# Rows of the modulated layer norm in two vector passes, and the last attention groups' gate steps in the MLP's third to fifth turns

## The reference

```python
ada = t_emb @ w_ada + b_ada
sh_msa, sc_msa, g_msa, sh_mlp, sc_mlp, g_mlp = jnp.split(ada, 6, axis=-1)
xn = layer_norm(logmap0(x))
xm = expmap0(xn * (1 + sc_msa) + sh_msa)
... attention over 16 heads ...
x = mobius_add(residual, expmap0(g_msa * logmap0(attn_out)))
xn = layer_norm(logmap0(x))
xm = expmap0(xn * (1 + sc_mlp) + sh_mlp)
ff = plin(plin(xm, w_f1, b_f1), w_f2, b_f2)
return mobius_add(residual, expmap0(g_mlp * logmap0(ff)))
```

## Time and profile before

| | us |
|---|---|
| median of 3 runs | 1152.47 (1149.03 to 1152.67) |
| the profiled execution's own time | 1151.27 |
| its span, first to last instruction | 1149.4 |
| PE busy | 999.6 (87%) |
| DVE busy | 964.9 (84%) |
| ACT busy | 854.4 (74%) |
| POOL busy | 551.0 (48%) |

### The profile page before, as it was taken

How to read it: one execution, slowest core, us unless ns; L and a number is a source line. 1 busy time by engine, 2 the same in 40 slices (tenths; PEclk the granted TensorE clock), 3 DMA queues, 4 the chain that set the end, 5 groups by cost and what they waited for, 6 DMA issues and landing times.

```text
span 1149.4 us, 23488 instructions
## 1 busy us (share of the span) xinstructions
PE 999.6 (87%) x7666; PEld 647.6 (56%) x7688; DVE 964.9 (84%) x2211; ACT 854.4 (74%) x2322; POOL 551.0 (48%) x1009
## 2 busy tenths in 40 slices
PE   7999987887699279999999999999885688889876
PEld 7888873333355146666666666666552355455544
DVE  5888777999488867899998999999878799999983
ACT  3545548887797246888888888888778888888872
POOL 2344424554387432444444444444204576677763
PEclk9999998999599689999999999999997799999998
DMA  7111201341699643454554444442373555766634
GB/s 245 46 49 55 61 22 63 127 171 79 215 354 326 186 109 93 111 124 123 131 127 123 113 111 111 112 112 69 83 176 68 101 130 147 183 157 165 156 95 125
DMA packets 113676, 148.16 MB, mean 129 GB/s; under 512 B 9232, under 2 KB 99472, under 8 KB 112784
## 3 DMA queue, kind: packets, MB, share of 16 engines
q1 hardware_dynamic: 113008, 146.64, 46.8%
q10 hardware_dynamic: 544, 0.00, 0.0%
HBM read 111.22 MB, written 27.00 MB: 120 GB/s over the span
## 4 chain that ended last, share of the span: by engine, by line
PE 22%; issue 12%; ACT 12%; DVE 7%; POOL 6%; DMA 4%; SPq 2%; DVEq 0%; POOLq 0%; ACTq 0%
PE t_fB L2053 6%; POOL t_qk L1971 4%; PE t_bk L2022 4%; PE t_fA L2053 3%; PE t_bk L1386 3%; DMA t_qbd<-t_qt 3%; PE t_fB L1407 2%; SPq L1856 2%; ACT t_ysq L2192 1%; ACT t_junk L1425 1%; ACT t_vbd L1467 1%; ACT t_vbd L1451 1%; DVE t_qt L1619 1%; PE t_bk L2103 1%; ACT t_qt L2306 1%
## 5 line engine op out<-in xcount | busy, mean ns | idle before, releaser
L1386 PE MATMUL t_bk<-k_w12g,t_ut 128*128 128x512 f32 x256 | 126.3, 617 | 3.2 <-DVE t_y L1589 2.4
L412 POOL TENSOR_SCALAR s_hleak<-k_hs,k_leak 128x128 f32<-128x128 f32 x126 | 46.9, 372 | 96.2 <-ACT k_hs L367 96.2
L2053 PE MATMUL t_fA<-k_wqkv,t_ut 128*128 128x512 f32 (+1 forms) x256 | 91.2, 499 | 1.5 <-ACT t_ut L2162 1.5
L2053 PE MATMUL t_fB<-k_wqkv,t_ut 128*128 128x512 f32 (+1 forms) x256 | 90.9, 498 | 0.0
L285 PE MATMUL s_gsum<-k_hs,k_w0t 128*128 128x128 f32 x504 | 77.6, 297 | 6.8 <-ACT k_hs L367 0.8
L2022 PEld LDWEIGHTS t_bk<-t_qbd,t_kpar 64*128 64x128 f32 x1024 | 62.8, 189 | 31.6 <-ACT t_pt L2198 10.7
L2022 PE MATMUL t_bk<-t_qbd,t_kpar 64*128 64x128 f32 x1024 | 75.2, 287 | 6.2 <-DMA t_qbd<-t_qt 1.8
L1386 PEld LDWEIGHTS t_bk<-k_w12g,t_ut 128*128 128x128 f32 x256 | 50.4, 198 | 53.3 <-issue 49.6
L745 ACT ACTIVATE a_silu<-a_pg,k_wxscale 128x512 f32<-128x512 f32 x96 | 64.9, 694 | 17.5 <-PE a_pu L710 17.3
L285 PEld LDWEIGHTS s_gsum<-k_hs,k_w0t 128*128 128x128 f32 x504 | 65.6, 190 | 20.6 <-ACT k_hs L367 20.1
L364 ACT ACTIVATE s_gate<-s_gsum,k_b 128x128 f32<-128x128 f32 x128 | 40.1, 363 | 45.7 <-PE s_gsum L285 45.7
(11 more groups left out here) (388 smaller groups left out, 2910.1 us busy)
## 6 DMA issues: line engine op xcount, KB each, us to landing
t_scb<-g_rows SPq DMA_DIRECT2D x64, 256.0 KB, 4.8
t_shb<-g_rows SPq DMA_DIRECT2D x64, 256.0 KB, 5.9
hidden_rows<-k_own SPq DMA_DIRECT2D x6, 1536.0 KB, 6.0
t_qbd<-x_rows SPq DMA_DIRECT2D x17, 512.0 KB, 6.3
s_xrow<-in_x_dram SPq DMA_DIRECT2D x16, 512.0 KB, 3.6
b_xin<-in_x_dram SPq DMA_DIRECT2D x16, 512.0 KB, 4.5
x_rows<-b_xout SPq DMA_DIRECT2D x16, 512.0 KB, 6.6
t_xf<-x_rows SPq DMA_DIRECT2D x16, 512.0 KB, 5.6
```

The source lines that it names most:

```text
L1386: last = nc.tensor.matmul(z.fW[:, j, :], z.ut[:, c, j * P:(j + 1) * P], k["w12g"][:, c, :], start=False, stop=(c == C - 1))
L2053: last = nc.tensor.matmul(dst[:, w0:w1], ut[:, c, j * P:(j + 1) * P], k["wqkv"][:, c, w0:w1], start=(c == 0), stop=(c == C - 1))
```

## The change

Rows: u is made as (x - m) * sc and then a * that + sh, each pass as four scalar_tensor_tensor of 128x256, in `norm` and `modulate`; `shift` is gone. `u_ready` counts tiles, `um_ready` is gone, and SP's loads wait on the new counts. In attention the same is done for group 0 only, and its first pass stands between the steps of the layer-norm factors. Lists: in turn(16) and in MLP turns 2 to 4, attention's closing stages of groups 14 and 15 and some of groups 0 to 3 are put in other places on DVE, ACT and POOL.

```diff
@@ -1242,7 +1242,7 @@
 
 MLP_SMALL = ("un2", "lu", "ru", "su", "quad", "q2", "lq", "rq", "s1", "yn2", "ly", "ry", "sy", "sy2", "an2", "am2", "xa",
              "la", "rn", "n", "e", "l1", "inv", "ld", "iden", "rsy", "xs", "w", "om", "den", "th", "top", "k", "A", "B")
-MLP_SIGNALS = ("sc_loaded", "sh_loaded", "gb_loaded", "xin_loaded", "stored", "xh_ready", "um_ready", "u_ready",
+MLP_SIGNALS = ("sc_loaded", "sh_loaded", "gb_loaded", "xin_loaded", "stored", "xh_ready", "u_ready",
                "un_ready", "act_u", "su_ready", "us_ready", "utp_ready", "ut_ready", "w_ready", "quad_ready", "guard_ready", "act_q", "s1_ready",
                "y2_ready", "yn_ready", "act_y", "sy_ready", "a_ready", "xa_ready", "an_ready", "am_ready", "act_tail",
                "pool_sy", "pool_pre", "pool_gate", "pool_top", "den_ready", "mob_ready",
@@ -1418,8 +1418,8 @@
 
     def norms_u(self, g):
         nc, act, z, s, S = self.nc, self.act, self.z, self.s, self.z.S
-        act.wait_ge(s["u_ready"], g + 1)
         for j in range(GT):
+            act.wait_ge(s["u_ready"], g * GT + j + 1)
             if g >= 1 or j:
                 act.wait_ge(s["un_ready"], g * GT + j)
             nc.scalar.activation(z.junk[0], z.u[g % 2][:, j, :], ACT.Square, accum_out=z.sc["un2"][:, j:j + 1]).then_inc(s["un_ready"], 1)
@@ -1550,11 +1550,12 @@
         assert c.n == 8
 
     def modulate(self, g):
-        nc, dve, z, s = self.nc, self.dve, self.z, self.s
-        u = z.u[g % 2]
+        nc, dve, k, z, s = self.nc, self.dve, self.k, self.z, self.s
         dve.wait_ge(s["xh_ready"], (g + 1) * GT)
-        dve.wait_ge(s["sc_loaded"], (g + 1) * 32)
-        nc.vector.tensor_tensor(u, u, z.scb[:, :, :], ALU.mult).then_inc(s["um_ready"], 1)
+        dve.wait_ge(s["sh_loaded"], (g + 1) * 32)
+        for j in range(GT):
+            nc.vector.scalar_tensor_tensor(z.u[g % 2][:, j, :], z.u[g % 2][:, j, :], k["ln"][:, g * GT + j, 0:1], z.shb[:, j, :],
+                                           ALU.mult, ALU.add).then_inc(s["u_ready"], 1)
 
     def quads(self, g):
         nc, dve, k, z, s, S = self.nc, self.dve, self.k, self.z, self.s, self.z.S
@@ -1658,16 +1659,10 @@
             dve.wait_ge(s["utp_ready"], g - 1)
         if g == NORMED and self.t:
             dve.wait_ge(t["ln_b"], 1)
+        dve.wait_ge(s["sc_loaded"], (g + 1) * 32)
         for j in range(GT):
-            nc.vector.tensor_scalar(z.u[g % 2][:, j, :], z.x1_row(g, j), k["ln"][:, g * GT + j, 0:1], k["ln"][:, g * GT + j, 1:2],
-                                    ALU.mult, ALU.add).then_inc(s["xh_ready"], 1)
-
-    def shift(self, g):
-        nc, dve, z, s = self.nc, self.dve, self.z, self.s
-        u = z.u[g % 2]
-        dve.wait_ge(s["um_ready"], g + 1)
-        dve.wait_ge(s["sh_loaded"], (g + 1) * 32)
-        nc.vector.tensor_tensor(u, u, z.shb[:, :, :], ALU.add).then_inc(s["u_ready"], 1)
+            nc.vector.scalar_tensor_tensor(z.u[g % 2][:, j, :], z.x1_row(g, j), k["mv"][:, g * GT + j, 0:1], z.scb[:, j, :],
+                                           ALU.subtract, ALU.mult).then_inc(s["xh_ready"], 1)
 
 def attention_mlp(nc, dr, k, out):
 
@@ -1812,11 +1807,11 @@
                     sp.dma_start(dst[h * T:(h + 1) * T, :, :], gate_rows(k["g_dram"][ADA_ROWS.index(part)], g, h)).then_inc(zs[loaded], 16)
 
             def second_scale(g):
-                sp.wait_ge(*((zs["um_ready"], g) if g else (s["um_ready"], NG)))
+                sp.wait_ge(*((zs["xh_ready"], g * GT) if g else (s["um_ready"], NG)))
                 second_rows(z.scb, 4, g, "sc_loaded")
 
             def second_shift(g):
-                sp.wait_ge(*((zs["u_ready"], g) if g else (s["u_ready"], NG)))
+                sp.wait_ge(*((zs["u_ready"], g * GT) if g else (s["u_ready"], NG)))
                 second_rows(z.shb, 3, g, "sh_loaded")
 
             def second_gate(g):
@@ -1978,8 +1973,9 @@
             once(second.clip_u, 1)
             scaled_norms(NG - 2)
             gate_step(NG)
-            scaled_y(NG)
             for i in range(NG + 4):
+                if i == 2:
+                    once(second.clip_u, 2)
                 once(second.scaled_norms, i - 2)
                 once(second.products, i - 4)
                 once(second.clip_u, i)
@@ -1987,10 +1983,12 @@
                 once(second.gate_step, i - 2)
                 once(second.quotients, i - 3)
                 once(second.factors, i - 2)
-                if i == 2:
+                if i == 3:
+                    scaled_y(NG)
                     scaled_norms(NG - 1)
+                once(second.clip_y, i - 1)
+                if i == 3:
                     gate_step(NG + 1)
-                once(second.clip_y, i - 1)
 
         @block.tensor
         def _(pe):
@@ -2320,7 +2318,7 @@
             norms_u(0)
             for i in range(NG):
                 turn(i)
-            gates = {2: turn(NG), 3: turn(NG + 1)}
+            gates = {2: turn(NG), 4: turn(NG + 1)}
             for i in range(NG + 5):
                 if i == 6:
                     scales_b.scalar_norms(act)
@@ -2337,11 +2335,18 @@
                 once(second.turned_u, i - 1)
                 if i in gates:
                     gates[i]["tanh_parts"]()
+                if i == 3:
+                    gates[2]["squares_yo"](NG)
+                once(second.norms_y, i - 2)
                 if i == 2:
-                    gates[i]["squares_yo"](NG)
-                once(second.norms_y, i - 2)
+                    once(second.norms_u, 2)
                 if i in gates:
                     gates[i]["inverse"]()
+                if i == 2:
+                    once(second.scaled_u, 2)
+                else:
+                    once(second.norms_a, i - 2)
+                if i in gates:
                     gates[i]["scaled_a"]()
                 once(second.norms_a, i - 2)
                 once(second.scaled_a, i - 3)
@@ -2350,9 +2355,18 @@
 
         @block.vector
         def _(dve):
+            def first_rows(j):
+                nc.vector.scalar_tensor_tensor(u[:, j, :], xf[:, j, :], k["mv"][:, j, 0:1], scb[:, j, :], ALU.subtract, ALU.mult).then_inc(s["xhat_ready"], 1)
+
             scales.vector_squares(dve)
+            dve.wait_ge(s["xf_loaded"], 16)
+            dve.wait_ge(s["sc_loaded"], 32)
+            first_rows(0)
+            first_rows(1)
             scales.vector_quotient(dve)
+            first_rows(2)
             scales.vector_scale(dve)
+            first_rows(3)
             scales.vector_norm(dve)
             dve.wait_ge(s["const_ready"], 1)
             second = MlpOnVector(nc, dve, k, z, zs, s)
@@ -2434,14 +2448,12 @@
                 if i == NG:
                     once(second.norm, 0)
                     once(second.modulate, 0)
-                    once(second.shift, 0)
                     outputs(0)
-                    once(second.norm, 1)
                     outputs(1)
                     gated()
+                    once(second.norm, 1)
+                    outputs(2)
                     once(second.modulate, 1)
-                    outputs(2)
-                    once(second.shift, 1)
                     outputs(3)
                     output_sums()
                     return {"moved": moved, "moments": moments}
@@ -2522,17 +2534,17 @@
                     scales_a.vector_norm(dve)
 
             dve.wait_ge(s["ln_x"], 1)
-            dve.wait_ge(s["xf_loaded"], 16)
+            dve.wait_ge(s["sh_loaded"], 32)
             for j in range(GT):
-                nc.vector.tensor_scalar(u[:, j, :], xf[:, j, :], ln_of(0, j, 0), ln_of(0, j, 1), ALU.mult, ALU.add).then_inc(s["xhat_ready"], 1)
-            modulate(0)
-            dve.wait_ge(s["um_ready"], 1)
-            dve.wait_ge(s["sh_loaded"], 32)
-            nc.vector.tensor_tensor(u[:, :, :], u[:, :, :], shb[:, :, :], ALU.add).then_inc(s["u_ready"], 1)
+                dve.wait_ge(s["xhat_ready"], j + 1)
+                rows = nc.vector.scalar_tensor_tensor(u[:, j, :], u[:, j, :], ln_of(0, j, 0), shb[:, j, :], ALU.mult, ALU.add)
+                if j == 0:
+                    rows.then_inc(s["um_ready"], 1)
+            rows.then_inc(s["u_ready"], 1)
             second.split_bias(flat_o[0:1, 0:3 * D], flat_ot[0:1, 0:3 * D // 2].bitcast(BF16))
             for i in range(NG):
                 turn(i)
-            gates = {2: turn(NG), 3: turn(NG + 1)}
+            gates = {2: turn(NG), 4: turn(NG + 1)}
             for i in range(NG + 5):
                 if i == 5:
                     scales_b.vector_squares(dve)
@@ -2542,17 +2554,20 @@
                     scales_b.vector_scale(dve)
                 if i == 11:
                     scales_b.vector_norm(dve)
-                if i == 3:
-                    gates[i]["gated"]()
                 once(second.quads, i - 2)
                 once(second.moved, i - 4)
                 once(second.norm, i)
                 once(second.maxima, i - 4)
                 once(second.outer, i - 2)
+                if i == 2:
```

(8 more changed lines are left out.)

## The result

| | before | after |
|---|---|---|
| median us (executions, lowest to highest) | 1152.57 (4, 1149.03 to 1153.06) | 1169.24 (4, 1162.80 to 1170.30) |
| ratio, 95% interval | 1 | 1.0137, 1.0101 to 1.0174 |
| profiled span, mean granted clock | 1149.4, 0.949 | 1166.8, 0.941 |

A forecast was written before the change was run, and what follows sets the result against it. No engine was full; in MLP turns DVE's list and a two-turn trip through ACT and PE were equally late. Terms 3.5 + 7.0 - 2.2 = 8.3 us gave 1159.6 profiled, 1160.8 us as median; range 1150.5 to 1165.5.

The forecast's parts named there:

- The head: Start of the second block: DVE waits for scale rows, GpSimd's memset holds `L1153`, u is ready 3.5 us later.
- The hand-over: Attention to MLP, turns 2 to 4: 5.5 us gained, 12.5 lost in turn 4, so y2(3) comes 7.0 us later.
- ACT's first wait: Turn 4: ACT waits 3.4 us at tanh_parts for GpSimd's am of attention group 15.
- the 20.3 of the sum: Turn 3: DVE alone is late, its listed work from y2 to the next y2 adding up to 20.3 us.
- The steady turns: MLP turns: DVE's list falls by 0.52 us a turn, the two-turn trip grows by 0.29; 2.2 us gained overall.
- the forecast 8.3: Whole kernel: head, hand-over and steady turns together make it 8.3 us slower.
- The trip: MLP cycle of quad, moved, norm, maxima, y2, ACT and PE: two turns long, 31.08 us after the change, 30.79 before.
- the one that steps y2 forward: MLP from turn 5: y2 at the later of previous + 14.87 + inserted work and two before + 31.08; 3.0 us gained.
- a microsecond in turn 11: MLP turn 11: the old trace lost about a microsecond to PE's low clock level; the new one may too.
- The bound of +1.5 us: Steady turns, slow end: 0.15 us lost in each of ten turns and nothing gained.
- DVE idle 0.5 us before the fourth quad, turns of 15.5 us: Sign for the steady MLP turns: DVE waits 0.5 us before the fourth quad, turns take 15.5 us.
- Rival 3 (rows held by GpSimd): Norm and modulate collide with GpSimd, at most 0.3 us a turn: 1164.8 us, chance 0.08.

The follow-up runs named there:

- e2: The kernel before with only the MLP's rows in two passes, head and lists unchanged: 1158.90 us, ratio 1.0055.
- e1: The changed kernel with the head of before, the rest as changed: 1166.19 us, ratio 1.0115.
- e8: e2 with 16 useless transposes a turn on PE ahead of its wait for the scaled rows: 1144.61 us, ratio 0.9923.
- e11: The changed kernel with only GpSimd's order in its turn 3 changed, attention's closing steps put earlier: 1161.02 us, ratio 1.0108.
- e3: The kernel before with only the list moves, rows still in three passes: 1161.47 us, ratio 1.0075.
- e6: e2 with norm moved behind gated in DVE's list for turns from 4 on: 1143.18 us, ratio 0.9920.
- e5: The changed kernel with the first row's gate sum taken three times a turn on DVE: 1174.27 us, ratio 1.0185.

## Why the prediction was wrong, step by step

- **The head, +3.5 us: right.** DVE waits 5.70 us for the scale rows and `L1153` is held 2.53 us in the memset, as written; 3.3 us in the traces, 2.5 by the ratios. PE's first transposes start 0.75 us later than before, and the memset beside them 2.57 us earlier, for the code ahead of the head ran that much sooner in this execution.
- **The hand-over, +7.0 us: right in mechanism, near in size, and that partly by luck.** By the traces 5.4 us (59.4 to 64.8), of which the rows alone give -1.0 (58.4 in e2) and the moves 6.7; by the ratios of e1 and e2 the moves cost 6.9. y2(2) to y2(3) is 26.3 us where the steps gave 29.6, since ACT's first wait was 1.65 and not 3.4, and DVE's 7.04 and not 10; y2(1) to y2(2) took 21.8 and not the 20.3 of the sum, for a tensor_scalar of DVE (`L1580`) was held 1.63 us beside GpSimd's quotients. The two misses go against each other, and that is the luck.
- **The steady turns, -2.2 us: wrong, and more than the whole of the error.** From y2(3) to y2(13) the forecast was 156.9 us, the trace has 168.7, before had 159.9: +8.8 us in place of -2.2. The two turns behind, for which nothing was forecast, add 3.0. The miss of 11.0 us and these 3.0 stand against 9.1 by which the difference of the spans, 17.4, exceeds the forecast 8.3; the other parts together came out below their forecast. The instruction costs were right (norm and modulate rows 1.58 us, list 14.83 us where I had 14.87). The trip was right too: 31.1 to 31.5 us in e8 and in the pair of e11. The step that failed is the one that steps y2 forward as the later of (previous + 14.87) and (two before + 31.08). It gives unequal turns, 14.9 and 16.2 us, and I took the trip's length as the same, 31.08 us, whatever the spacing; what the runs show in its place is a pair of 34.0 us. With that spacing PE's idle time of a pair comes in one piece, 1.82 us twice in before's steady turns and 3.29 once here, and the clock falls behind it, which makes the trip 2.8 us longer. The prediction mentioned this cost once, as a microsecond in turn 11, and priced it at nothing elsewhere. The bound of +1.5 us for this term was the sum of a lengthened trip and no more.
- **DVE idle 0.5 us before the fourth quad, turns of 15.5 us** was the sign named for the steady part. It showed at once that the step was wrong: 1.50 us before three quads, in every second turn.
- **Rival 3 (rows held by GpSimd)** ends near the measured time and is still not the cause: every four rows of norm or modulate in the steady turns take 1.66 or 1.67 us. Where they lie beside GpSimd's small steps it is rather these that are longer: two steps of `L1206` beside the norm rows take 0.32 us, the next two, behind those rows, 0.20 (1041.76 to 1042.83 of the changed kernel).

The Trainium skill, page "TensorE: Matmul & The Clock Gate", section "HAM oscillation — how this bites in real kernels", describes a matmul loop in which a wait comes back each round, there for a DMA, and the array starts each round slow. It was the page to weigh against this change; the rows above agree with it: 1.94 us against 1.07 for the same eight transposes, behind the same wait in successive pairs. It was not so every time, as e11 shows.

Does it add up? By the ratios: rows in the MLP +6.3 us, the moves +6.9, the head +2.5, together 15.7, and the whole change is 15.8 (1.37% of 1152). That these agree proves nothing, for each is the difference of one kernel to the next. The moves measured by themselves (e3) cost 8.6 us, so the parts aren't quite independent. In the traces: head 3.3, hand-over 5.4, y2(3) to y2(15) 11.9, the rounds behind it 0.6, less 3.8 in stretches ahead of them (2.6 us ahead of the head, and 1.2 between PE's first transposes and y2(0), a stretch that lies between 464.7 and 467.6 us in the thirteen traces, so that this much is chance), together 17.4, the difference of the spans.

## What to carry to other kernels

When a list is shortened in a loop that a longer cycle also bounds, step the turns forward and look at where the idle time of the other engines gathers, not only at its sum: here 0.5 us taken from VectorE's turn put TensorE's idle time into one stretch and cost 1.0 us a turn. Take the instruction off the cycle before you make it cheaper; without useless matmuls the two-pass rows gained (0.8%) only when norm stood outside the stretch from quads to y2. A cheap test of whether an idle TensorE costs anything but its idle time is to give it useless work just ahead of the wait.

## What the hardware showed that I had not expected

- Idle stretches of the same length don't always cost the clock. From y2(3) on, the changed kernel, e1, e2 and e11 have 23 waits of 3.29 to 3.74 us before turn_u; behind 20 of them the clock fell, in turn_u or in the mixed pass, and behind 3 it didn't. Single cases: 3.29 us before turn_u and the lower level behind it (after), 3.30 us and the upper level (e11); 2.31 us and the lower level once in e3, 2.32 us and the upper level in before. Shorter ones can cost it too: behind 1.82 us in before's steady turns it never fell, but in an early turn of e6 it fell behind 1.59 us with 0.46 just before it. The fall can also come after PE has resumed: in e11, 2.56 us of idle time, turn_u at 1.07 us, then two groups of the mixed pass at 1.80 and 1.88. What decides these runs don't show.
- Work added to one engine can move another's idle time by way of a third: 0.95 us a turn on VectorE delayed GpSimd's xd step, for which TensorE then waited 0.97 us, where it had not waited before (e5). The whole of it, some 15 us of added work, cost 5.5 us by the ratios, whose intervals overlap.
